# Attention layer 0: projection begun inside the last head, the next batch's transposes between its tiles; feed-forward stage written without a loop

## The chip, the cores and the metric

The kernel runs on one core of a Trainium2 chip. The metric is the device time in microseconds (us); the kernel before ran in 2813.58 us, the median of three runs (2812.09 to 2816.76). The core has a matrix engine (TensorE, PE in rows), three elementwise engines (VectorE or DVE, ScalarE or ACT, GpSimd or POOL) and a queue engine (SP) that issues most transfers. PE reads from SBUF and writes only into PSUM, here 8 banks of 128 x 512 fp32. DVE and ACT read and write both memories; GpSimd works in SBUF alone here.

## The reference, cut to what matters

Input x is 4 sequences (B) of 1024 tokens (T) of 512 features (D). Layer 0 is attention between two conditioned LayerNorms; layer 1 is attention and a feed-forward block whose weights are ternary and whose activations are rounded to 8 bits.

```python
# layer 0, for each of 4 sequences; 16 heads of 32
h   = gamma * layernorm(x) + beta                   # "front": gamma, beta from the condition
q, k, v = split(h @ Wqkv.T + bqkv)
out = (softmax(q @ k.T) / D ** 0.5) @ v
h1  = out @ Wp.T + bp + x                           # projection and residual
x   = gamma * layernorm(h1) + beta + h1             # "tail"
# layer 1
x = x + bitlinear(attention(bitlinear(adaln(x))), w_proj, b_proj)
x = x + bitlinear(gelu(bitlinear(adaln(x), w_fc1, b_fc1)), w_fc2, b_fc2)
```

## The kernel before

Three functions run one after the other: `layer0`, `layer1a` (attention of layer 1) and `layer1b` (feed-forward). Each engine has its own instruction stream, written out in Python; an engine works its stream strictly in order, and a `wait_ge` on a semaphore holds everything behind it.

`layer0` goes over the 4 batches b. In each: 16 units of q and k and 8 of v (L995, 12 matmuls each, made of high and low fp32r parts `h_hi`, `h_lo` of the front's output); then 16 heads (`Attention.run_pe`, `run_act`, `run_dve`, `run_pool`: `loop` calls `head` for k = 0 to 16, each with steps s = 0 to 7). In step s of head k PE computes two 128 x 512 score tiles (L428, PSUM banks 0 to 2 in a ring), ACT takes their exponentials (L508), and PE computes chunks of the row maxima for a head ahead (L414, banks 3 to 5, reduced by DVE at L547). There are none of these chunks left after step 1 of head 14, so banks 3 to 5 are free from there. Behind step 2 and inside step 6 come the products with the values (L448, banks 6 and 7), a copy by ACT (L517), 16 tiny matmuls that fold and transpose (L455) and the division by DVE (L564, L566), which puts a head's output into `tok`. POOL sums exponentials (L368, L374); four of the sums of a last pair are DVE's (L385, L390).

After the heads comes what this document calls the boundary. PE transposes `tok` (eight units of 4 transposes of 128 x 128, L1030), ACT and DVE copy half of them each into `oT` (L1144, L1440), and PE projects: 8 token tiles t, each of 4 matmuls k over 128 features, that is four heads each (L1037), into PSUM bank t. For each tile DVE adds the residual (L1451), computes the LayerNorm statistics (L1468, L1472) and their inverse root (L1454, L1456), ACT normalises (L1150), DVE multiplies by gamma (L1465), POOL adds beta to h1 (L908) and DVE adds both (L1475) into `xs`, which SP stores. POOL adds the bias `bp` to the residual ahead of it (L902). The semaphore `s_x1` counts the finished tiles. Then the front of the next batch: its input `xn` (normalised by DVE, L1202) is transposed by PE into eight PSUM banks (L936, units n = 4c + k for token half c and feature quarter k), each as soon as the tail has left that bank; ACT and DVE turn each into `h_hi` (L1061 and L1058), a full-precision copy in place (L1063 on ACT for c = 0, `exact`, L1209, on DVE for c = 1) and `h_lo` (L1216, function `rest`). ACT also takes squares of `xs` (L1083) and absolute sums of weight pieces (L1078) in this time. In the last batch there is no next front; instead the tail goes on with layer 1's first RMSNorm and its quantisation (L1459, L1478, L911, L1296).

`layer1b` goes over 32 tiles of 128 tokens as a software pipeline: `steps` calls a list of stages (offset, function) for each step n, in the order of the list. Steps n = -6 to 1 and 26 to 33 are written out; steps 2 to 25 are a loop of 6 rounds of 4 steps, in which n is a register and every slice that depends on n has an address computed at run time. In a step DVE finds the largest |h| (L2157, 2048 wide), makes six 128 x 1 values (L2164, L2176, L2170), turns matmul results into h (L2191, twice), rounds (L2181, L2198) and adds the residual (L2204); ACT scales and rounds (L2112, L2126), takes Gelu (L2122, twice), makes 8-bit values (L2131), scales a later tile (L2106) and copies (L2116); POOL modulates that later tile (L2047, L2051) and adds a bias (L2054).

## Time and profile before

| | |
|---|---|
| median of three runs | 2813.58 us |
| the profiled execution's own time | 2812.82 us |
| its span, first to last instruction | 2811.0 us |
| PE busy | 2632.5 us, 94% |
| DVE busy | 2185.9 us, 78% |
| ACT busy | 1826.0 us, 65% |
| POOL busy | 1922.1 us, 68% |
| mean granted TensorE clock | 0.981 of full speed |

A row of the timeline gives the start, the time taken, the engine, the source line and operation, what is written and read, and how many instructions are merged; in square brackets stands the idle time of the engine before it and what ended that. PE's matmuls are pipelined, so their durations overlap and the pace is read from the starts. In the rows fp32 data of 512 columns appears as two instructions per matmul, so the 32 matmuls of the projection are 64.

### The profile page before, as it was taken

Reading aid. Unit: us, or ns where it says so; the run is one execution under the profiler, and the core shown is the slowest. Engines: PE = TensorE matmul, PEld = TensorE weight load, DVE = VectorE, ACT = ScalarE, POOL = GpSimd, SP = SyncE. Lnnn points to the kernel's source line nnn. Section 1 sums busy time; section 2 is a strip of 40 time slices with the busy share of each in tenths; the row PEclk is TensorE's granted clock in tenths of the full one; section 3 lists DMA queues with packets and bytes.
Section 4 is the critical chain, followed back from the end, with each engine's and each line's share of the span. In section 5 each row is a group of like instructions: output and inputs, shape, how many; then the busy total and the mean of one; then the engine's idle time right before and its main releaser. Section 6 shows DMA issues by size and latency. Waiting matters only on the chain. (4 is left out here: it accounts for less than half of the span.)

```text
span 2811.0 us, 60795 instructions
## 1 busy us (share of the span) xinstructions
PE 2632.5 (94%) x21761; PEld 1461.6 (52%) x21761; DVE 2185.9 (78%) x4491; ACT 1826.0 (65%) x3298; POOL 1922.1 (68%) x1547
## 2 busy tenths in 40 slices
PE   7899999999999999999859998999899999987998
PEld 5655466554665547555325554555455445533443
DVE  5777678777887778877567778777877787758997
ACT  4366654665556655666556677667766776667886
POOL 0289724897259962699548986987789788965442
PEclk9999999999999999999979999999999999999999
DMA  6122443224432335223232313321432232245444
GB/s 233 39 58 58 143 127 114 58 58 147 129 97 62 85 116 164 74 58 103 75 80 53 85 34 106 81 59 31 117 81 58 50 99 58 59 181 162 100 101 108
DMA packets 168754, 260.29 MB, mean 93 GB/s; under 512 B 85388, under 2 KB 91668, under 8 KB 167576
## 3 DMA queue, kind: packets, MB, share of 16 engines
q1 hardware_dynamic: 166680, 250.27, 32.6%
q0 software_dynamic: 1792, 6.33, 0.6%
q8 instruction: 169, 2.77, 0.4%
q14 instruction: 113, 0.93, 0.1%
HBM read 99.15 MB, written 38.88 MB: 49 GB/s over the span
## 5 line engine op out<-in xcount | busy, mean ns | idle before, releaser
L547 DVE TENSOR_REDUCE a_mxs<-ps 128x1 f32<-128x512 f32 x2048 | 1268.8, 682 | 258.1 <-PE ps L414 255.7
L508 ACT ACTIVATE a_p<-ps 128x512 f32<-128x512 f32 x2048 | 1043.1, 605 | 204.3 <-PE ps L428 194.3
L368 POOL TENSOR_TENSOR a_sum<-a_p 128x512 f32<-128x512 f32 x736 | 939.9, 1287 | 204.0 <-PE ps L448 123.4
L414 PE MATMUL ps<-a_k,a_q 96*128 96x512 f32 x2048 | 856.3, 425 | 24.5 <-DVE a_mxs L547 20.9
L428 PE MATMUL ps<-a_q,a_k 98*128 98x512 f32 x2048 | 810.0, 418 | 18.5 <-ACT a_p L508 11.5
L448 PE MATMUL ps<-a_sum,a_unit 128*32 128x512 f32 x1536 | 654.0, 598 | 3.0 <-POOL a_sum L368 3.0
L374 POOL TENSOR_TENSOR a_sum<-a_sum,a_p 128x512 f32<-128x512 f32 x480 | 618.8, 1289 | 37.6
L448 PE MATMUL ps<-a_p,xv 128*32 128x512 f32 x3968 | 642.5, 598 | 0.0
L414 PEld LDWEIGHTS ps<-a_k,a_q 96*128 96x128 f32 x2048 | 389.8, 190 | 258.6 <-DVE a_mxs L547 105.5
L428 PEld LDWEIGHTS ps<-a_q,a_k 98*128 98x128 f32 x2048 | 384.1, 189 | 258.1 <-ACT a_p L508 162.0
L517 ACT ACTIVATE a_ots<-ps 128x512 f32<-128x512 f32 x256 | 152.8, 598 | 397.5 <-PE ps L448 396.4
L448 PEld LDWEIGHTS ps<-a_sum,a_unit 128*32 128x32 f32 x1536 | 135.6, 110 | 164.8 <-issue 129.1
L448 PEld LDWEIGHTS ps<-a_p,xv 128*32 128x32 f32 x3968 | 165.3, 110 | 101.3 <-issue 69.8
L564 DVE RECIPROCAL a_rec<-ps 128x4 f32<-128x4 f32 x256 | 45.2, 176 | 138.3 <-PE ps L455 138.3
L455 PEld LDWEIGHTS ps<-a_fold,a_ots 128*32 128x32 f32 x8192 | 98.4, 111 | 88.9 <-issue 85.0
L2074 PE MATMUL ps<-b_next_w,c_xqT 128*128 128x512 bf16 x512 | 118.7, 386 | 22.1 <-DVE c_h L2191 20.1
L2085 PE MATMUL ps<-b_next_w,c_hT 128*128 128x512 bf16 x512 | 117.2, 383 | 7.8 <-DVE b_next_x L2204 6.4
L455 PE MATMUL ps<-a_fold,a_ots 128*32 128x33 f32 x8192 | 118.9, 198 | 2.1 <-ACT a_ots L517 2.1
L2047 POOL TENSOR_TENSOR c_tk<-c_tk,b_next_mod 128x512 f32<-128x512 f32 x32 | 40.5, 1266 | 115.5 <-ACT c_tk L2106 115.5
L1037 PE MATMUL ps<-qh,ql 128*128 128x512 f32 x256 | 110.8, 593 | 3.3 <-ACT ql L1144 3.3
L908 POOL TENSOR_TENSOR kh<-kh,qh 128x512 f32<-128x512 f32 x32 | 40.6, 1270 | 83.4 <-ACT ps L1150 72.7
L2074 PEld LDWEIGHTS ps<-b_next_w,c_xqT 128*128 128x128 bf16 x512 | 48.2, 99 | 91.0 <-DVE c_h L2191 26.5
(251 smaller groups left out, 3049.1 us busy)
## 6 DMA issues: line engine op xcount, KB each, us to landing
a_q<-qh SPq DMA_DIRECT2D x256, 128.0 KB, 2.3
a_k<-kh SPq DMA_DIRECT2D x256, 128.0 KB, 2.4
a_q<-ql SPq DMA_DIRECT2D x128, 128.0 KB, 2.3
a_k<-kl SPq DMA_DIRECT2D x128, 128.0 KB, 2.4
x<-a_p SPq DMA_DIRECT2D x64, 256.0 KB, 2.1
a_p<-in_w_fc SPq DMA_DIRECT2D x12, 1024.0 KB, 8.0
kh<-in_x SPq DMA_DIRECT2D x4, 2048.0 KB, 14.4
a_p<-x SPq DMA_DIRECT2D x16, 512.0 KB, 5.8
```

The source lines that it names most:

```text
L368: pair = pool.tensor_tensor(tile, keys[0], keys[1], ALU.add)
L374: pool.tensor_tensor(tile, tile, keys[2], ALU.add).then_inc(self.s_sum, 1)
L414: pe.matmul(self.mx[self.mx_ring[at]], self.q[j][0:96, t * P:(t + 1) * P], self.k[j][0:96, half * HALF:(half + 1) * HALF], start=True, sto ...
L428: pe.matmul(self.st[self.st_ring[at]], self.k[j][0:98, kt * P:(kt + 1) * P], self.q[j][0:98, u * HALF:(u + 1) * HALF], start=True, stop=Tr ...
L448: mm = pe.matmul(self.ot[half % 2][HD * c:HD * (c + 1), :], weights, tile, start=r == rounds[0], stop=r == rounds[-1])
L455: mm = pe.matmul(self.ot[u][HD * c:HD * (c + 1), t * (HD + 1):(t + 1) * (HD + 1)], self.ots[:, u, t * P + HD * c:t * P + HD * (c + 1)], se ...
L508: act.activation(self.key_tile(u, kt), self.st[self.st_ring[CHUNKS * k + n]], ACT.Exp, scale=self.scale).then_inc(self.s_exp, 1)
L517: act.activation(self.ots[:, u, :], self.ot[u], ACT.Copy).then_inc(self.s_ots, 1)
L547: dve.reduce_max(self.mxs[:, k % 2, c:c + 1], self.mx[self.mx_ring[CHUNKS * k + c]], axis=AX.X).then_inc(self.s_mxr, 1)
L1037: mm = pe.matmul(ps[:, t, :], oT[:, k, t * P:(t + 1) * P], wp[:, k, :], start=k == 0, stop=k == KC - 1)
L2074: mm = pe.matmul(f1[:, j, :], xqT[:, r % 2, k, :], w1[:, k, j * HALF:(j + 1) * HALF], start=k == 0, stop=k == KC - 1)
L2085: mm = pe.matmul(f2, hT[:, r % 2, k, :], w2[:, k, :], start=k == 0, stop=k == FC - 1)
```

## The change

1. In heads 14 and 15 PE transposes six of the eight units of `tok` (`tokens`, those of heads 0 to 11) into banks 3 to 5, between score tiles, and DVE copies them to `oT` (`extra` in DVE's stream). From step 4 of head 15 to the end of the loop PE does seven matmuls of the projection (`projected`). The last two units of `tok` follow behind the loop, with two more matmuls between them; ACT copies these two, and its `roots` now comes before them.
2. The projection's tiles go to other banks (`Y_BANK`), and so do the next q, k and v units. From tile 3 on, PE puts one transpose unit of the next batch's front behind each tile; the front uses banks 3, 4, 5, 0, 3, 4, 5, 1, and its units wait for the multiplication by gamma (`s_gm`) or for `rest` of the unit before in that bank. ACT now makes the full-precision copy for all eight units, DVE's `exact` is only for batch 0. ACT and DVE begin on the front at t = 4 and t = 6 of the tail's loop.
3. The multiplication by gamma now writes `xs` out of PSUM, and the last addition of the tail is POOL's.
4. `layer1b` writes all steps out; the order of the stages in a step stays.

```diff
+        s_gm = sem("gamma")
         s_rr, s_xr, s_vl = sem("root_inv"), sem("x_rooted"), sem("v_last")
-        tail_home = lambda b, t: ps[:, t, :] if t < 6 or b == B - 1 else xs[:, t, :]
         UN = 2 * KC
+        Y_BANK = (3, 4, 5, 0, 1, 2, 6, 7)
+        tail_home = lambda b, t: ps[:, Y_BANK[t], :] if t < 6 or b == B - 1 else xs[:, t, :]
+        FRONT_BANK = lambda b: (3, 4, 5, 0, 3, 4, 5, 1) if b else tuple(range(UN))
+        TOKENS = [(k, c) for c in range(2) for k in range(KC - 1)] + [(KC - 1, 0), (KC - 1, 1)]
+        T_BANK = (3, 4, 5, 3, 4, 5, 6, 7)
+        EARLY = len(TOKENS) - 2
+        TOKENS_AT = {(14, 4): 0, (14, 5): 1, (14, 7): 2, (15, 0): 3, (15, 1): 4, (15, 3): 5}
+        COPIED_AT = {(14, 5): 0, (14, 6): 1, (15, 0): 2, (15, 1): 3, (15, 2): 4, (15, 4): 5}
+        PART_AT = {(15, 4): ((0, 0),), (15, 5): ((0, 1),), (15, 7): ((0, 2),), (16, 0): ((1, 0),), (16, 1): ((1, 1),),
+                   (16, 2): ((1, 2),), (16, 6): ((2, 0),)}
...
-                    for t in range(TT + 4 if last else TT):
+                    for t in range(TT + 4 if last else TT + 1):
                         if t < TT:
                             pool.wait_ge(s_zt, TT * b + t + 1)
+                            pool.wait_ge(s_xb, TT * b + t + 1)
                             pool.tensor_tensor(h1[:, t, :], h1[:, t, :], mod_r[:, 1, :], ALU.add).then_inc(s_hb, 1)
+                        if 1 <= t <= TT:
+                            pool.wait_ge(s_gm, TT * b + t)
+                            pool.wait_ge(s_hb, TT * b + t)
+                            pool.tensor_tensor(xs[:, t - 1, :], xs[:, t - 1, :], h1[:, t - 1, :], ALU.add).then_inc(s_x1, 1)
...
-                        if prior is not None:
-                            if n < 6:
-                                pe.wait_ge(s_x1, TT * prior + n + 1 + 1)
-                            else:
-                                pe.wait_ge(s_h1, TT * prior + n + 1)
+                        if b and n < 4:
+                            pe.wait_ge(s_gm, TT * (b - 1) + n + 1)
+                        elif b and n < 7:
+                            pe.wait_ge(s_trD, UN * b + n - 4 + 1)
+                        elif b:
+                            pe.wait_ge(s_gm, TT * (b - 1) + Y_BANK.index(FRONT_BANK(b)[n]) + 1)
                         for i in range(4):
-                            mm = pe.transpose(ps[:, n, i * P:(i + 1) * P], xn[:, 4 * c + i, k * P:(k + 1) * P], ident)
+                            mm = pe.transpose(ps[:, FRONT_BANK(b)[n], i * P:(i + 1) * P], xn[:, 4 * c + i, k * P:(k + 1) * P], ident)
                         mm.then_inc(s_tr, 1)
+
+                def tokens(b, i):
+                    k, c = TOKENS[i]
+                    if i == 0:
+                        pe.wait_ge(att.s_mxr, CHUNKS * H * (b + 1) + att.MX_CREDIT)
+                    if i < EARLY:
+                        pe.wait_ge(att.s_o, 2 * H * b + 2 * NJ * (KC - 1) + 2)
+                    else:
+                        pe.wait_ge(att.s_o, 2 * H * (b + 1) + c + 1)
+                    if 3 <= i < EARLY:
+                        pe.wait_ge(s_opD, EARLY * b + i - 3 + 1)
+                    for n in range(4):
+                        mm = pe.transpose(ps[:, T_BANK[i], n * P:(n + 1) * P], tok[:, 4 * c + n, k * P:(k + 1) * P], ident)
+                    mm.then_inc(s_op, 1)
+
+                def projected(b, t, k):
+                    if (t, k) == (0, 0):
+                        pe.wait_ge(s_late, 48 * (b + 1))
+                    if t < 3 and k == 0:
+                        pe.wait_ge(s_opD, EARLY * b + 3 + t + 1)
+                    if (t, k) == (3, 0):
+                        pe.wait_ge(att.s_exp, CHUNKS * H * (b + 1) + att.EXP_CREDIT)
+                    if (t, k) == (4, 0):
+                        pe.wait_ge(s_opD, EARLY * (b + 1))
+                    if t >= 6 and k == 0:
+                        pe.wait_ge(s_opA, 2 * b + t - 6 + 1)
+                    if t in (0, 4) and k == KC - 1:
+                        pe.wait_ge(s_opA, 2 * b + t // 4 + 1)
+                    mm = pe.matmul(ps[:, Y_BANK[t], :], oT[:, k, t * P:(t + 1) * P], wp[:, k, :], start=k == 0, stop=k == KC - 1)
+                    if k == KC - 1:
+                        mm.then_inc(s_y, 1)
...
-                    att.run_pe(pe, b)
-                    pe.wait_ge(att.s_o, 2 * H * (b + 1) + 2)
-                    for n, (c, k) in enumerate(HALVES):
-                        for i in range(4):
-                            mm = pe.transpose(ps[:, n, i * P:(i + 1) * P], tok[:, 4 * c + i, k * P:(k + 1) * P], ident)
-                        mm.then_inc(s_op, 1)
-                    pe.wait_ge(s_opA, KC * (b + 1))
-                    pe.wait_ge(s_opD, KC * (b + 1))
-                    pe.wait_ge(s_late, 48 * (b + 1))
+                    def extra(k, s):
+                        if (k, s) in TOKENS_AT:
+                            tokens(b, TOKENS_AT[k, s])
+                        for t, c in PART_AT.get((k, s), ()):
+                            projected(b, t, c)
+                    att.run_pe(pe, b, extra)
+                    tokens(b, EARLY)
+                    projected(b, 2, 1)
+                    tokens(b, EARLY + 1)
+                    projected(b, 2, 2)
                     for t in range(TT):
-                        for k in range(KC):
-                            mm = pe.matmul(ps[:, t, :], oT[:, k, t * P:(t + 1) * P], wp[:, k, :],
-                                           start=k == 0, stop=k == KC - 1)
-                        mm.then_inc(s_y, 1)
+                        for c in range(KC - 1 if t < 3 else 0, KC):
+                            projected(b, t, c)
+                        if not last and t >= 3:
+                            front(b + 1, (t - 3,))
                     if not last:
-                        front(b + 1, b)
+                        front(b + 1, range(5, UN))
...
+                        to, at = h_hi[:, k, c * HALF:(c + 1) * HALF], ps[:, FRONT_BANK(b)[n], :]
+                        if c and b == 0:
+                            act.wait_ge(s_trG, k + 1)
+                            act.activation(to, at, ACT.Copy).then_inc(s_trA, 1)
                             continue
                         act.wait_ge(s_tr, UN * b + n + 1)
-                        act.activation(to, ps[:, n, :], ACT.Identity,
+                        act.activation(to, at, ACT.Identity,
                                        bias=mod_col(b, 1, k), scale=mod_col(b, 0, k)).then_inc(s_trA, 1)
-                        act.activation(ps[:, n, :], ps[:, n, :], ACT.Identity,
+                        act.activation(at, at, ACT.Identity,
...
-                    for n, (c, k) in enumerate(HALVES):
-                        if k % 2 == 0:
-                            act.wait_ge(s_op, UN * b + n + 1)
-                            act.activation(oT[:, k, c * HALF:(c + 1) * HALF], ps[:, n, :], ACT.Copy).then_inc(s_opA, 1)
                     if not last:
                         roots(b + 1)
+                    for i in range(EARLY, len(TOKENS)):
+                        k, c = TOKENS[i]
+                        act.wait_ge(s_op, len(TOKENS) * b + i + 1)
+                        act.activation(oT[:, k, c * HALF:(c + 1) * HALF], ps[:, T_BANK[i], :], ACT.Copy).then_inc(s_opA, 1)
...
-                        if not last and t == 6:
-                            modulate(b + 1, range(2))
+                        if not last and 4 <= t:
+                            modulate(b + 1, (t - 4,))
                     if not last:
-                        modulate(b + 1, range(2, UN))
+                        modulate(b + 1, range(5, UN))
                         act.wait_ge(s_wsum, done(b + 1) + 2)
...
+                    def extra(k, s):
+                        if (k, s) in COPIED_AT:
+                            i = COPIED_AT[k, s]
+                            n, c = TOKENS[i]
+                            dve.wait_ge(s_op, len(TOKENS) * b + i + 1)
+                            dve.tensor_copy(oT[:, n, c * HALF:(c + 1) * HALF], ps[:, T_BANK[i], :]).then_inc(s_opD, 1)
+                    att.run_dve(dve, b, spare, extra)
...
-                        if t >= TT and not last:
-                            modulate(b + 1, t - TT)
                         if 2 <= t < TT + 2:
-                            home = tail_home(b, t - 2)
                             dve.wait_ge(s_zt, TT * b + t - 1)
-                            cht.mark(dve.tensor_tensor(home, home, mod_r[:, 0, :], ALU.mult))
+                            dve.tensor_tensor(xs[:, t - 2, :], tail_home(b, t - 2), mod_r[:, 0, :], ALU.mult).then_inc(s_gm, 1)
+                        if t >= 6 and not last:
+                            rest(b + 1, t - 6)
                         if t < TT:
                             dve.wait_ge(s_h1, TT * b + t + 1)
                             cht.mark(dve.bn_stats(st1[:, t, :], h1[:, t, :]))
-                        if t < TT + 2:
+                        if t < TT:
                             cht.wait_alone()
-                        if t < TT:
                             dve.bn_aggr(mv[1][:, t, :], st1[:, t, :]).then_inc(s_var1, 1)
-                        if 2 <= t < TT + 2:
-                            dve.wait_ge(s_hb, TT * b + t - 1)
-                            dve.tensor_tensor(xs[:, t - 2, :], home, h1[:, t - 2, :], ALU.add).then_inc(s_x1, 1)
                         if last and 5 <= t < TT + 5:
                             dve.wait_ge(s_xr, t - 5 + 1)
-                            dve.tensor_tensor(xv[:, t - 5, :], ps[:, t - 5, :], g1[:, 0, :], ALU.mult).then_inc(s_n1, 1)
...
+                    if not last:
+                        for n in range(4, UN):
+                            rest(b + 1, n)
...
-        def steps(eng, stages, before_loop=lambda: None):
-
-            def step(n, r, every):
+        def steps(stages, before_third=lambda: None):
+
+            for n in range(FIRST, N + 2):
+                if n == 2:
+                    before_third()
                 for o, f in stages:
-                    if every or 0 <= n + o < N:
-                        f(n + o, (r + o) % UNROLL)
-            for n in range(FIRST, 2):
-                step(n, n % UNROLL, False)
-            before_loop()
-            with eng.Fori(0, LOOPS) as i:
-                for r in range(UNROLL):
-                    step(UNROLL * i + 2 + r, (2 + r) % UNROLL, True)
-            for n in range(2 + UNROLL * LOOPS, N + 2):
-                step(n, n % UNROLL, False)
+                    if 0 <= n + o < N:
+                        f(n + o, (n + o) % UNROLL)
```

PE at the end of batch 0, from the last step of head 15 to the first q unit. `a_q`, `a_k` rows are scores, `a_p`, `a_sum` rows products with values, `ps<-ident,tok` transposes of `tok`, `ps<-qh,ql` the projection (the two names are the memory of Wp and `oT`), `ps<-ident,kl` the next front. Before:

```order
L455 MATMUL ps<-a_fold,a_ots 32x33 x32
L1030 MATMUL ps<-ident,tok 128x128 x32
L1037 MATMUL ps<-qh,ql 128x512 x32
L936 MATMUL ps<-ident,kl 128x128 x32
L995 MATMUL ps<-a_h_hi,a_q 128x512 x4
```

and in the changed kernel, in two pieces, the steps of head 15 from step 3 and then what follows the last products with values:

```order
L428 MATMUL ps<-a_q3,a_k3 128x512 x2
L967 MATMUL ps<-ident,tok 128x128 x4
L428 MATMUL ps<-a_q3,a_k3 128x512 x2
L983 MATMUL ps<-qh,ql 128x512
L428 MATMUL ps<-a_q3,a_k3 128x512 x2
L983 MATMUL ps<-qh,ql 128x512
L428 MATMUL ps<-a_q3,a_k3 128x512 x2
```

```order
L455 MATMUL ps<-a_fold,a_ots 32x33 x16
L983 MATMUL ps<-qh,ql 128x512
L967 MATMUL ps<-ident,tok 128x128 x4
L983 MATMUL ps<-qh,ql 128x512
L967 MATMUL ps<-ident,tok 128x128 x4
L983 MATMUL ps<-qh,ql 128x512 x8
L953 MATMUL ps<-ident,kl 128x128 x4
L983 MATMUL ps<-qh,ql 128x512 x4
L953 MATMUL ps<-ident,kl 128x128 x4
```

Seven projection matmuls and six transpose units stand between the last heads' matmuls, and only the last four front units (16 transposes) are behind the projection. On DVE, tile 7 of the tail in batch 0 read before (the row of L1451 is the residual, the last one the addition that goes to POOL):

```order
L1451 TENSOR_TENSOR kh<-ps,kh 128x512
L1454 RECIPROCAL a_rs1<-a_sd1 128x1
L1456 TENSOR_SCALAR a_nm<-a_mv1,a_rs1 128x1
L1465 TENSOR_TENSOR ps<-ps,qh 128x512
L1468 BN_STATS a_st1<-kh 128x6
L1472 BN_AGGR a_mv1<-a_st1 128x2
L1475 TENSOR_TENSOR a_p<-ps,kh 128x512
```

and reads now, with what each waits for:

```order
L1507 TENSOR_TENSOR kh<-ps,kh 128x512 [waits a_xb,a_y]
L1510 RECIPROCAL a_rs1<-a_sd1 128x1 [waits a_sd1_ok]
L1512 TENSOR_SCALAR a_nm<-a_mv1,a_rs1 128x1 [waits a_v_tail]
L1518 TENSOR_TENSOR a_p<-ps,qh 128x512 [waits a_zt]
L1270 TENSOR_TENSOR a_h_lo_75<-ps,a_h_hi_76 128x4x128 [waits a_trF,a_trA]
L1523 BN_STATS a_st1<-kh 128x6 [waits a_h1]
```

The last addition is gone from DVE's tile, and one `rest` of the next front stands in its place.

## Rows read from the trace of the kernel before

**Rows 1.** Timeline of PE, batch 0, from the last products to the next q unit

```profile
340.66 0.59 PE L448 MATMUL ps<-a_sum,a_unit 128*32 128x512 f32 x1 [0.59 <-POOL a_sum L368]
...
343.53 3.71 PE L1030 MATMUL ps<-ident,tok 128*128 128x128 f32 x32 [0.64 <-DVE tok L566]
348.07 27.70 PE L1037 MATMUL ps<-qh,ql 128*128 128x512 f32 x64 [0.83 <-ACT ql L1144]
...
383.20 1.19 PE L995 MATMUL ps<-a_h_hi,a_q 128*128 128x512 f32 x4 [2.67 <-ACT a_h_hi L1061]
```

**Rows 2.** Timelines of PE and ACT in head 15, eight score tiles

```profile
323.41 0.96 PE L428 MATMUL ps<-a_q,a_k 98*128 98x512 f32 x3
324.66 2.46 PE L428 MATMUL ps<-a_q,a_k 98*128 98x512 f32 x5 [0.28 <-ACT a_p L508]
...
324.02 4.02 ACT L508 ACTIVATE a_p<-ps 128x512 f32<-128x512 f32 x8
```

**Rows 3.** Timeline of DVE, heads 14 and 15 and boundary of batch 0

```profile
321.97 1.70 DVE L385 TENSOR_TENSOR a_sum<-a_p 128x512 f32<-128x512 f32 x1
...
327.80 0.29 DVE L566 SCALAR_TENSOR_TENSOR tok<-ps,a_rec 128x128 f32<-128x128 f32 x1
...
349.23 4.60 DVE L1202 TENSOR_SCALAR kl<-kl,a_mv,a_rs 128x512 f32<-128x512 f32 x8
...
364.54 0.66 DVE L1475 TENSOR_TENSOR a_p<-ps,kh 128x512 f32<-128x512 f32 x1
```

**Rows 4.** Timeline of ACT, boundary of batch 0

```profile
365.51 1.91 ACT L1078 ACTIVATE a_ots<-a_p 128x2048 bf16<-128x2048 f32 x1
...
376.25 0.78 ACT L1061 ACTIVATE a_h_hi<-ps,a_mod_p 128x512 fp32r<-128x512 f32 x1 [0.46 <-PE ps L936]
376.93 0.74 ACT L1063 ACTIVATE ps<-ps,a_mod_p 128x512 f32<-128x512 f32 x1
```

**Rows 5.** Timeline of DVE, tail of the last batch, its first and last instruction

```profile
1375.91 0.69 DVE L1451 TENSOR_TENSOR kh<-ps,kh 128x512 f32<-128x512 f32 x1 [3.87 <-PE ps L1037]
...
1415.82 0.69 DVE L1296 TENSOR_REDUCE a_am<-xv 128x1 f32<-128x512 f32 x1 [0.54 <-POOL xv L911]
```

**Rows 6.** Windows: length, PE, PEld, DVE, ACT, POOL busy, granted clock, DMA

```profile
333.00:338.00 5.00, 5.00 (x52) 1.47 (x51) 1.86 (x4) 1.68 (x4) 2.66 (x3) 0.66 0.01 3
```

**Rows 7.** Timeline of DVE, feed-forward: the loop's first step and the first step behind it

```profile
2567.25 2.29 DVE L2157 TENSOR_REDUCE c_am<-c_h 128x2048 f32 x1 [0.39 <-ACT c_h L2122]
...
2756.94 2.27 DVE L2157 TENSOR_REDUCE c_am<-c_h 128x1 f32<-128x2048 f32 x1
...
2762.07 1.27 DVE L2181 TENSOR_SCALAR c_xq<-c_tk 128x512 bf16<-128x512 f32 x1
...
2763.85 0.90 DVE L2198 TENSOR_SCALAR c_hq<-c_h 128x512 bf16<-128x512 f32 x1
...
2765.33 2.27 DVE L2157 TENSOR_REDUCE c_am<-c_h 128x1 f32<-128x2048 f32 x1
```

**Rows 8.** Timeline of ACT, feed-forward, from the loop into the written-out steps

```profile
2752.38 0.72 ACT L2112 ACTIVATE c_tk<-c_tk,c_am 128x512 f32<-128x512 f32 x1 [0.93 <-DVE c_am L2170]
...
2759.75 0.72 ACT L2112 ACTIVATE c_tk<-c_tk,c_am 128x512 f32<-128x512 f32 x1 [0.40 <-DVE c_am L2170]
...
2762.27 1.99 ACT L2122 ACTIVATE c_h<-c_h 128x1024 f32<-128x1024 f32 x2
```

**Rows 9.** Timelines of DVE, ACT and POOL in written-out steps ahead of the loop

```profile
2557.55 0.42 DVE L2181 TENSOR_SCALAR c_xq<-c_tk 128x512 bf16<-128x512 f32 x1
...
2564.91 1.02 DVE L2181 TENSOR_SCALAR c_xq<-c_tk 128x512 bf16<-128x512 f32 x1
...
2557.75 1.99 ACT L2122 ACTIVATE c_h<-c_h 128x1024 f32<-128x1024 f32 x2
...
2564.37 1.28 POOL L2054 TENSOR_TENSOR b_next_x<-b_next_x,b_next_b 128x512 f32<-128x512 f32 x1
```

**Rows 10.** Timeline of DVE at the end of the kernel

```profile
2802.18 0.75 DVE L2204 SCALAR_TENSOR_TENSOR b_next_x<-ps,c_am,b_next_x 128x512 f32<-128x512 f32 x1 [3.78 <-issue]
```

69 lines of the change are left out of this document (33 added, 36 removed).

## The prediction

> **What bounds the kernel now.** The page comes first: PE is busy for 94% of the span, so what frees PE counts and what adds to it costs, except where PE only seems busy. The timeline of PE at the end of a batch shows the first such place. In batch 0 the last product waits 0.59 us for POOL's sum, the transposes 0.64 us for DVE, the projection 0.83 us for ACT, and the first q unit 2.67 us for ACT's `h_hi` [rows 1]. From that last product's wait to the q unit at 383.20 are 42.5 us, of which the projection is 27.5 (64 instructions, 0.43 us apart, so 0.86 us a matmul and 3.44 a tile) and the eight units of `tok` 3.7 (0.46 us each) [rows 1]. The other boundaries repeat these figures.
>
> The second place is inside head 15. PE's rows for eight score tiles start at 323.41 and end at about 327.05: 3.64 us. The first three are issued some 0.24 us apart, so eight need 1.9 us; the other five come at ACT's pace, whose eight exponentials take 4.02 us [rows 2]. PE shows as busy and has 1.7 us to spare in such a group. There are three of them from head 14, step 3 on, where no maxima are left to compute: 5.2 us a batch.
>
> The third is the feed-forward stage. Its 24 looped steps run from 2567.25 to 2756.94, 7.90 us each [rows 7]. What limits them is a ring, not one engine: ACT rounds h and does Gelu, DVE takes the maximum and the small factors, ACT goes on. In the loop ACT's L2112, which heads the ring, starts after 0.93 us of waiting for DVE's L2170 [rows 8].
>
> **Part 1: work moved into the heads.** Six transposed units (6 x 0.46 = 2.8 us) and seven matmuls (7 x 0.86 = 6.0 us) leave the boundary. Two units fall into the first group and three into the second: 0.9 and 1.4 us, under the 1.7 to spare, and free, since PE may be three tiles ahead of ACT. The third group gets one unit and two matmuls, 2.2 us, 0.5 too much. Three more matmuls (2.6 us) stand ahead of the last products, where PE waited 0.59 us before: net 2.0. So the folds, which began at 341.5, begin at 344.0. From there PE does two folds (0.3 us each), two units (0.9), seven matmuls to the end of tile 2 (6.0), and five tiles of 3.44 with a front unit of 0.46 behind each (19.5): 371. The last three front units end at 372.5. That is PE's own floor, 10.7 us under 383.20.
>
> DVE must keep up in head 15. The division there ended at 328.1 [rows 3]. Four copies of 0.6 us now stand ahead of it. Idle stretches of 0.4 to 0.5 us absorb some; the sum L385, which took 1.70 us because POOL was in a sum of its own [rows 3], ends at the same moment when it starts later; 0.7 us is left. The division ends at 328.8, and the product that needs it starts at 329.05, two rounds of 0.86 us behind the fold: nothing is added, by 0.2 us.
>
> **Part 2: the front's chain.** DVE goes through a tile in 3.44 us at PE's pace; without L1475 (0.6) and a wait of 0.3 it is 2.5 us. It begins behind the normalisation, 4.60 us [rows 3], at about 351, with three tiles waiting, and has caught up at tile 5. PE's first front unit waits 1 us for gamma; tile 7 ends at 371.5. ACT is what is late next: each of the eight units now takes L1061 and L1063, 1.33 us [rows 4], where four took 0.5 us for a copy. With normalisation, root and square it has 2.9 us of work a tile, and in two tiles 2.1 us more for L1078 [rows 4]. Taken tile by tile: DVE has the statistics of tile 7 at 374.6; ACT squares and modulates unit 3 until 376.9 and normalises tile 7 until 377.6; PE's front units 6 and 7 wait for `rest` of unit 2 (377.1) and end at 378.1, where the q unit starts. The last `rest` (383.6) is needed by the third q unit at 385.4: hidden, by 1.8 us. POOL has two operations of 1.27 us in 3.9 us; its lateness moves stores and squares only. So 383.20 becomes 378.1, and 0.2 us of waiting inside the first q unit goes: **5.3 us at each of three boundaries, 16 us**. The bounds are PE's floor, 10.7 us each, and nothing, if ACT and DVE hold PE until the old time.
>
> DVE's multiplication by gamma for tiles 6 and 7 reads two SBUF operands while POOL runs. The nearest row is L385, 1.70 us against 0.66 for L1475 with POOL idle [rows 3]; the schedule has 0.6 us for each. The Trainium skill (SBUF — State Buffer, section "SBUF: two separate sides") says that such a DVE operation and a GpSimd one take a shared port pair exclusively, so that one waits out the other; the row agrees. By that rule alone each could wait out a whole POOL operation, and the sum would be some 4 us smaller over three boundaries.
>
> **Part 3: the last batch.** DVE bounds its tail: 40.6 us from the first residual to the last maximum [rows 5]. Tiles 0 to 2 now come some 6 us earlier. A full tile takes DVE 3.7 us without the addition of 0.6, and POOL, with three operations, 3.8: POOL becomes the pace. Gone through in the same way, the last maximum comes 6.8 us earlier: **7 us**. Bounds: 4, if POOL is held up at each tile, to 10.
>
> **Part 4: the feed-forward stage.** L2164, L2176 and L2170 write through computed addresses in the loop. From the loop into the written-out steps ACT's L2112 follows after 7.37 us, not 7.90, and its wait falls from 0.93 to 0.40 [rows 8]. So a ring of 7.4 us is shown. DVE alone needs 7.06: the step from 2756.94 to 2765.33 without the 0.85 and 0.48 us that L2181 and L2198 took too long [rows 7, 9]. L2181 also meets POOL's third operation: POOL's ended at 2565.65, L2181, begun at 2564.91, at 2565.93, and took 1.02 us instead of 0.42 [rows 9]. POOL's third ends 5.9 us behind the Gelu [rows 9], and the Gelu ends 7.3 us after the maximum's start [rows 7, 8]; so in steps of S it ends at 13.2 - S into the next, L2181 0.3 us behind it, and DVE has 1.6 more: S = 15.1 - S, or 7.55. That saves 24 x 0.35 = 8.5 us, and the first step behind them 0.4: **9 us**. Bounds: 12 (the ring alone) and nothing.
>
> The Trainium skill (Advanced Engine Details and Errata, "Control Flow Timing") gives a compare and branch 108 ns. By that the loop's six rounds cost under 1 us, and the sum would be 8 us smaller. The rows speak for more: the interval shortens within a step.
>
> **Part 5: the clock.** In head 15 of batch 0 the granted clock was 0.66 on average over 5 us, that is partly at the lower level, 1.2 GHz [rows 6], in products that follow tiles at ACT's pace; batch 3 has the same. Each cost some 1.6 us. PE now has work in those gaps. I count half: **1.6 us**.
>
> **Sum.** 16 + 7 + 9 + 1.6 = 33.5 us. The profiled execution took 2812.8, so 2779.3; the median of the runs is 0.8 higher: 2780.
>
> **Rivals.** (a) Without the loop only its branches are saved: 24.6 + 1 us, 2788. For it: the ring could be paced by more than the small operations. Against: rows 8. Chance 0.12. (b) The front's chain on ACT, or POOL in DVE's way, holds PE, and layer 0 gives half: 12 + 9, 2792. For it: only 1.8 us between the last `rest` and its need, 0.2 for the division. 0.13. (c) Layer 0 gives more: 10 us a boundary, near PE's floor, and both clock falls gone, 2764. 0.10. (d) Each feed-forward step meets POOL twice, as that of 8.39 us did [rows 7]: 24 x 0.49 = 12 us more than before in place of 9 less, 2801. Against: POOL had four additions in a row there, which only the steps behind the loop have. 0.04. (e) Slower: straight-line code arrives late. DVE stood 3.78 us near the end with no engine named [rows 10]. One such gap in each of 24 steps decides from 33.5 / 24 = 1.4 us; at 2 us the time is 2828. Against: layer 0 is straight-line already, and its q unit's 4 matmuls follow one another in 1.19 us [rows 1]. 0.03. The rest, 0.58, is the forecast, in 2774 to 2786.
>
> **Numbers.** A measurement of this kernel can tell about 0.2%, 5.6 us, from no change. The range leaves out (d), (e) and most of (c): 2769 to 2793. Faster 0.96, within 0.2% 0.01, slower 0.03.
>
> **What would show it.** The q unit 5 us nearer to the last heads, its wait for ACT gone; L2157's starts 7.5 to 7.6 us apart with L2181 at 0.7 to 1.0 us; the third score group of head 15 longer by 0.5 us, the others as before; the last maximum 7 us earlier. The prediction is wrong if PE waits for L566 in head 15, if front units wait for `rest` by more than 1 us each, or if steps stay at 7.9 us.

## The result, and the profile after

The changed kernel ran in 2795.3 us, the median of four runs (2792.4 to 2797.7), against 2814.4 for the kernel before on the same chip: a ratio of 0.9932, with a 95% interval of 0.9914 to 0.9949. It is faster, by 19 us. The prediction was 2780, in 2769 to 2793: the direction was right, and the gain nearly 60% of the 33.5 us forecast. The profiled execution took 2797.68 us, with a span of 2795.9: 15.1 us under the span before. It is the longest of the changed kernel's four runs (two are near 2797 us, two near 2793), so this pair of traces shows 4 us less than the medians; the working below goes by the pair. The page begins:

```profile
span 2795.9 us, 59973 instructions
PE 2621.9 (94%) x21716; PEld 1469.8 (53%) x21761; DVE 2162.2 (77%) x4455; ACT 1830.6 (65%) x3302; POOL 1964.9 (70%) x1579
```

Lines have moved: L1037 is now L983, L936 L953, L995 L1048, L1202 L1256, L1216 L1270, L902 L912, L1465 L1518, L2157 L2204, L2181 L2228. PE in the third group of score tiles of head 15, in batch 0:

```profile
330.77 0.74 PE L428 MATMUL ps<-a_q,a_k 98*128 98x512 f32 x2
331.35 0.60 PE L967 MATMUL ps<-ident,tok 128*128 128x128 f32 x4
...
333.68 1.02 PE L983 MATMUL ps<-qh,ql 128*128 128x512 f32 x2
334.14 1.04 PE L428 MATMUL ps<-a_q,a_k 98*128 98x512 f32 x2
335.11 0.46 PE L455 MATMUL ps<-a_fold,a_ots 128*32 128x33 f32 x32
```

From 330.77 to the folds (L455) are 4.34 us, where the group in [rows 2] took 3.64; the extra 0.7 us buys a transposed unit and two matmuls. This part went as forecast. The timeline of PE at the boundary, which answers to [rows 1], did not:

```profile
343.10 0.48 PE L455 MATMUL ps<-a_fold,a_ots 128*32 128x33 f32 x32
...
347.65 7.03 PE L983 MATMUL ps<-qh,ql 128*128 128x512 f32 x16
357.97 0.82 PE L953 MATMUL ps<-ident,kl 128*128 128x128 f32 x4 [3.28 <-DVE a_p L1518]
358.58 5.14 PE L983 MATMUL ps<-qh,ql 128*128 128x512 f32 x8
...
364.00 3.60 PE L983 MATMUL ps<-qh,ql 128*128 128x512 f32 x8
...
375.18 0.60 PE L953 MATMUL ps<-ident,kl 128*128 128x128 f32 x4
377.64 0.66 PE L953 MATMUL ps<-ident,kl 128*128 128x128 f32 x4 [1.86 <-DVE a_h_lo L1270]
380.45 1.97 PE L953 MATMUL ps<-ident,kl 128*128 128x128 f32 x8 [2.15 <-DVE a_h_lo L1270]
382.06 2.06 PE L1048 MATMUL ps<-a_h_hi,a_q 128*128 128x512 f32 x4
383.92 1.85 PE L1048 MATMUL ps<-a_h_hi,a_w_lo 128*128 128x512 f32 x4
385.61 1.08 PE L1048 MATMUL ps<-a_h_lo,a_q 128*128 128x512 f32 x4
```

The folds begin at 343.10 (forecast 344.0) and tile 3 is done before 355. Then PE stands 3.28 us for the first multiplication by gamma, and tile 4, eight instructions, takes 5.14 us where the next takes 3.60. The last front units wait 1.86 and 2.15 us for `rest`, and the q unit starts at 382.06, only 1.1 us earlier than before, with its first four matmuls in 2.06 us where they took 1.19. Its third group of matmuls starts at 385.61; before, it started at 385.59, so by then nothing is left of the gain. Windows of the same stretch (length, then PE, PEld, DVE, ACT and POOL busy, granted clock, DMA share and GB/s) show what the long rows are:

```profile
354.00:358.00 4.00, 0.72 (x3) 0.06 (x2) 3.64 (x12) 1.93 (x4) 1.26 (x1) 1.00 0.43 166
358.00:363.00 5.00, 5.00 (x11) 2.50 (x12) 2.88 (x8) 2.76 (x7) 4.88 (x4) 0.66 0.00 0
363.00:375.00 12.00, 12.00 (x38) 5.87 (x37) 7.66 (x19) 9.54 (x18) 5.07 (x5) 1.00 0.07 7
382.00:386.00 4.00, 4.00 (x12) 3.21 (x12) 2.63 (x5) 4.00 (x8) 3.72 (x3) 0.55 0.99 376
```

Behind the idle 354 to 358 the granted clock averages 0.66 over 5 us, and in the q unit 0.55 over 4, so it is partly at the lower level, 1.2 GHz. The trace of the kernel before has no such stretch at a boundary, though PE waits 1.03 and 2.67 us there: an idle gap is not enough by itself, as e11 and e12 show again below. DVE's timeline tells why gamma was late, with one row of POOL's beside it:

```profile
345.76 7.03 DVE L1256 TENSOR_SCALAR kl<-kl,a_mv,a_rs 128x512 f32<-128x512 f32 x8
352.70 0.68 DVE L1507 TENSOR_TENSOR kh<-ps,kh 128x512 f32<-128x512 f32 x1
...
357.14 0.68 DVE L1518 TENSOR_TENSOR a_p<-ps,qh 128x512 f32<-128x512 f32 x1
...
379.71 0.68 DVE L1270 TENSOR_TENSOR a_h_lo<-ps,a_h_hi 128x512 fp32r<-128x512 f32 x1
```

```profile
340.24 10.43 POOL L912 TENSOR_TENSOR kh<-kh,qh 128x512 f32<-128x512 f32 x8
```

The eight normalisations of the next input took 7.03 us, not 4.60 [rows 3], beside POOL's additions of `bp`. Tile 0's residual waited for them. The later boundaries repeat it: the q units start at 723.75 (before 724.45) and 1065.08 (before 1065.00). Over three boundaries and the batches between them nothing was gained. Taken apart: from the folds behind head 15 to the q unit are 38.9 us at each boundary, 2.8 less than before (41.69); the q unit's first two groups take 1.0 to 1.2 us more; and from the third group to the next batch's folds are 2.1 and 2.6 us more, the price of the matmuls that now stand in the heads (forecast 2.5).

The other two parts went as forecast. The last maximum of the last batch and the feed-forward maxima, both on DVE:

```profile
1409.13 0.69 DVE L1350 TENSOR_REDUCE a_am<-xv 128x1 f32<-128x512 f32 x1 [0.53 <-POOL xv L926]
...
2560.85 2.29 DVE L2204 TENSOR_REDUCE c_am<-c_h 128x1 f32<-128x2048 f32 x1 [0.26 <-ACT c_h L2169]
...
2606.04 2.27 DVE L2204 TENSOR_REDUCE c_am<-c_h 128x1 f32<-128x2048 f32 x1
...
2611.16 0.95 DVE L2228 TENSOR_SCALAR c_xq<-c_tk 128x512 bf16<-128x512 f32 x1
...
2741.27 2.27 DVE L2204 TENSOR_REDUCE c_am<-c_h 128x1 f32<-128x2048 f32 x1
2749.34 2.27 DVE L2204 TENSOR_REDUCE c_am<-c_h 128x1 f32<-128x2048 f32 x1
```

The last maximum comes 6.7 us earlier than in [rows 5]; as the q unit of this batch started no earlier, all of it was gained in the last batch. The 24 steps that were a loop take 180.42 us, 7.52 each (before 189.69, 7.90), and the step behind them 8.07, not 8.39 [rows 7].

The spans differ by 15.1 us: layer 0 (to its last maximum) 6.7 shorter, layer 1's attention 0.4 longer, from the first to the last 2048-wide maximum 9.7 shorter, and 0.9 longer behind it.

### The profile page after: what moved, and what is told of

The parts are those of the page before. It is cut to its first block and busy times, and to the rows that moved or that the text cites. A ratio compares the mean times of both kernels' runs of the same rounds, so it can differ in the third digit from the quotient of the medians.

```text
span 2795.9 us, 59973 instructions
## 1 busy us (share of the span) xinstructions
PE 2621.9 (94%) x21716; PEld 1469.8 (53%) x21761; DVE 2162.2 (77%) x4455; ACT 1830.6 (65%) x3302; POOL 1964.9 (70%) x1579
## 5 line engine op out<-in xcount | busy, mean ns | idle before, releaser
L455 PEld LDWEIGHTS ps<-a_fold,a_ots 128*32 128x32 f32 x8192 | 98.0, 110 | 90.2 <-issue 85.4
L983 PE MATMUL ps<-qh,ql 128*128 128x512 f32 x256 | 121.2, 612 | 0.0
L455 PE MATMUL ps<-a_fold,a_ots 128*32 128x33 f32 x8192 | 118.5, 198 | 0.4 <-ACT a_ots L517 0.4
L1731 POOL TENSOR_TENSOR xv<-xv,kh 128x512 f32<-128x512 f32 x32 | 40.4, 1277 | 71.3 <-ACT xv L1847 42.3
```

What stands on the lines that cost most here:

```text
L455: mm = pe.matmul(self.ot[u][HD * c:HD * (c + 1), t * (HD + 1):(t + 1) * (HD + 1)], self.ots[:, u, t * P + HD * c:t * P + HD * (c + 1)], se ...
L983: mm = pe.matmul(ps[:, Y_BANK[t], :], oT[:, k, t * P:(t + 1) * P], wp[:, k, :], start=k == 0, stop=k == KC - 1)
```

## Experiments

Two theories were tried against each other. A: the boundary is DVE's. The normalisation meets POOL, the tail starts late, PE's idle time is followed by a half clock, and the order of `rest` behind tile 7 sets the q unit. B: something else holds PE (the chain through ACT, the load of the chip), and DVE's start matters little. Each kernel is the changed one with the edit named (e12 is the kernel before with one); all but the changed one were timed beside the kernel before in one of three groups (2813.2, 2812.9 and 2812.8 us). The starts are from one trace of each.

| run | median us | ratio to before, 95% | folds to q unit, us (batches 0, 1, 2) | q unit of batch 1 | of batch 3 | last maximum of layer 0 |
|---|---|---|---|---|---|---|
| before | 2812.8 to 2813.2 | 1 | 41.7, 41.7, 41.7 | 383.20 | 1065.00 | 1415.82 |
| changed | 2795.3 | 0.9932 (0.9914 to 0.9949) | 39.0, 38.9, 38.9 | 382.06 | 1065.08 | 1409.13 |
| e1_bp_split | 2783.6 | 0.9895 (0.988 to 0.991) | 34.2, 34.2, 34.2 | 377.98 | 1050.64 | 1395.11 |
| e2_filler | 2786.1 | 0.9897 (0.9881 to 0.9912) | 36.5, 36.5, 36.5 | 379.55 | 1054.41 | 1397.97 |
| e3_ff_loop | 2809.3 | 0.9985 (0.9976 to 0.9994) | 39.0, 38.9, 38.0 | 384.68 | 1067.57 | 1413.12 |
| e4_norm_split | 2789.4 | 0.9913 (0.99 to 0.9927) | 36.4, 36.1, 35.8 | 380.93 | 1058.22 | 1401.72 |
| e5_shift | 2797.5 | 0.995 (0.9936 to 0.9963) | 38.5, 38.4, 38.4 | 382.27 | 1065.99 | 1410.84 |
| e6_no_part | 2788.3 | 0.9914 (0.9901 to 0.9928) | 38.0, 38.3, 38.6 | 378.44 | 1055.63 | 1401.41 |
| e7_split_filler | 2775.4 | 0.9868 (0.9853 to 0.9883) | 33.4, 33.4, 33.4 | 375.08 | 1044.13 | 1387.53 |
| e8_dve_add | 2802.2 | 0.9964 (0.995 to 0.9977) | 39.9, 41.0, 39.9 | 383.43 | 1069.10 | 1416.34 |
| e9_late_part | 2774.3 | 0.9869 (0.9852 to 0.9886) | 35.0, 35.0, 35.0 | 375.62 | 1044.38 | 1388.06 |
| e10_split_shift | 2769.8 | 0.9853 (0.984 to 0.9867) | 30.6, 30.6, 30.6 | 372.56 | 1037.80 | 1381.39 |
| e11_shift_only | 2783.5 | 0.9903 (0.9888 to 0.9918) | 33.7, 35.4, 35.4 | 378.15 | 1052.58 | 1395.72 |
| e12_ff_only | 2800.7 | 0.9968 (0.9955 to 0.9981) | 41.7, 41.7, 41.7 | 381.20 | 1065.57 | 1415.56 |

Ten of these kernels (all but before, e6, e9 and e12) have the same code up to the folds behind head 15 of batch 0, and yet these folds start anywhere from 341.70 (e7) to 345.66 us (e3). The start of a q unit carries this difference, the time from the folds to it does not.

### e1: POOL's additions out of the normalisation's way

```diff
                     for t in range(TT):
+                        if t == 4 and not last:
+                            pool.wait_ge(s_z, TT * (b + 2))
                         pool.tensor_tensor(h1[:, t, :], h1[:, t, :], bp, ALU.add).then_inc(s_xb, 1)
```

> POOL adds bp to four tiles, waits for DVE's eight normalisations, and adds it to the other four. Theory A (POOL's additions beside DVE's normalisation are what made it 7.03 us in place of 4.60; the first front unit's wait of 3.28 us and the half clock behind it follow from that): the normalisation takes 4.6 us again, the wait of the first front unit falls by 2.4 us to about 0.9, tile 4 takes 3.44 us and not 5.14, and the q units start 2.4 to 4.1 us earlier at each of three boundaries: 7 to 12 us off 2795. Theory B (the chain through DVE and ACT behind tile 7 sets the q unit, whatever the start of the tail): the wait of the first front unit falls too, but the last front units' waits of 1.86 and 2.15 us grow by as much; under 2 us in all.

Measured: 11.7 us faster than the changed kernel. DVE's row, then PE's two:

```profile
346.47 3.74 DVE L1258 TENSOR_SCALAR kl<-kl,a_mv,a_rs 128x512 f32<-128x512 f32 x8
```

```profile
355.57 0.63 PE L955 MATMUL ps<-ident,kl 128*128 128x128 f32 x4 [0.17 <-DVE a_p L1520]
...
373.55 0.66 PE L955 MATMUL ps<-ident,kl 128*128 128x128 f32 x4 [1.86 <-DVE a_h_lo L1272]
376.36 1.97 PE L955 MATMUL ps<-ident,kl 128*128 128x128 f32 x8 [2.15 <-DVE a_h_lo L1272]
```

The normalisation takes 3.74 us, 0.47 each, which is less than in the kernel before: there it met POOL's last additions too. The wait of 3.28 falls to 0.17 and the half clock behind it is gone: tile 4 takes 3.60 us. From the folds to the q unit are 34.2 us at all three boundaries, in place of 38.9. The waits of 1.86 and 2.15 us are unchanged to the hundredth, so they don't depend on when the tail starts. Theory B fell, for it wanted them longer. The low clock in the q unit stays too: its third group starts 2.53, 3.40 and 3.56 us behind its first in the three batches.

### e2 and e7: work in PE's idle time

Matmuls into banks that are overwritten later, `filler(bank, 3)` ahead of front unit 0 (e2 only) and `filler(bank, 2)` ahead of units 5 and 6, behind a wait (`s_h1`) until DVE has read the bank:

```diff
+                def filler(to, count):
+                    for i in range(count):
+                        pe.matmul(ps[:, to, :], oT[:, 0, 0:P], wp[:, 0, :], start=True, stop=True)
```

> The changed kernel with three idle-time matmuls on PE ahead of the first front unit and two each ahead of front units 5 and 6, into banks that are overwritten later; nothing else moves. Theory A (the two half-clock stretches at a boundary come from PE's idle time just before them): granted clock 1.00 in both stretches, tile 4 in 3.44 us (1.7 less), first q unit's twelve matmuls 2 us faster: 2 to 3.7 us at each boundary, 6 to 11 us in all. Theory B (the low clock has another cause, such as the load of the whole chip): the stretches stay, no gain, or up to 2 us loss from the seven matmuls where they outlast the waits.

> POOL's additions divided as in e1_bp_split, and two idle-time matmuls on PE ahead of front units 5 and 6, none ahead of unit 0. Theory A (the remaining half-clock stretch comes from the waits of 1.86 and 2.15 us): the stretch is gone at all three boundaries, last eight transposes in 1.1 and not 1.97 us, the first q unit's twelve matmuls 2 us faster: 2 to 3 us a boundary, 2774 to 2778. Theory B (the low clock follows from the load, not from the waits): 2783, as without.

The first q unit of batch 1 in e7:

```profile
375.08 1.18 PE L1054 MATMUL ps<-a_h_hi,a_q 128*128 128x512 f32 x4
...
377.03 1.09 PE L1054 MATMUL ps<-a_h_lo,a_q 128*128 128x512 f32 x4
```

The unit's third group starts 1.95 us behind its first; in the changed kernel 3.55 (382.06 to 385.61). Windows of e2 over the two places of low clock:

```profile
358.00:363.00 5.00, 5.00 (x18) 2.67 (x19) 3.77 (x12) 2.77 (x6) 4.94 (x4) 1.00 0.00 0
379.00:383.00 4.00, 4.00 (x23) 3.42 (x22) 2.58 (x4) 4.00 (x7) 3.45 (x4) 1.00 1.05 404
```

The clock stays at the upper level in both, with the other engines doing what they did. The useless matmuls make the kernel 9.2 us faster (e2), and 8.2 us faster on top of e1 (e7, forecast 2774 to 2778). Not all of the 8.2 is theirs: e7's first folds already start 2.1 us before e1's, in the same code, and the three boundaries with their q units give 6.0. So the low clock came with PE's idle time, and the load around it was not enough to bring it about.

### e4: half of the normalisation behind the tail's start

```diff
-                        normalize(ch, b + 1)
+                        normalize(ch, b + 1, range(4))
...
+                        if 3 <= t < TT - 1 and not last:
+                            normalize(ch, b + 1, (t + 1,))
```

> DVE normalises four tiles of the next input ahead of the tail and one each behind tiles 3 to 6, POOL's additions as in the changed kernel. The tail begins 3.5 us earlier (half of 7.03). Theory A: the first front unit's wait of 3.28 us is gone, tile 4 at full clock: 3 to 5 us at each boundary, 9 to 14 us in all, a little less where the late normalisations (0.6 us each) stand in DVE's chain. Theory B (the chain behind tile 7 sets the q unit): 0 to 2 us, or slower by the 0.6 us that stand between the statistics and the next residual.

Only 5.9 us were gained, where theory A wanted 9 to 14 and B at most 2. The first half did not take 3.5 us:

```profile
347.16 5.20 DVE L1257 TENSOR_SCALAR kl<-kl,a_mv,a_rs 128x512 f32<-128x512 f32 x4
```

Four normalisations beside POOL take 1.30 us each, and alone the same instruction takes 0.47 (e1). POOL's additions take 1.30 each here (10.43 for 8) and 1.24 where no normalisation runs beside them (4.97 for 4 in e1). DVE goes at POOL's pace, one instruction to an addition, as if each waited one out, and POOL loses little. This is the row that sizes the meeting.

### e5 and e11: the order of the front's work on ACT and DVE

e11 changes only the order, as below. e5 has e4's and e1's division too (POOL waits for four normalisations), and calls `rest` one step earlier still, for unit t - 4 from t = 4 on:

```diff
-                        if not last and 4 <= t:
-                            modulate(b + 1, (t - 4,))
+                        if not last and 3 <= t:
+                            modulate(b + 1, (t - 3,))
...
-                        if t >= 6 and not last:
-                            rest(b + 1, t - 6)
+                        if t >= 5 and not last:
+                            rest(b + 1, t - 5)
```

> DVE normalises four tiles ahead of the tail and one behind each of tiles 3 to 6; POOL adds bp to four tiles, waits for those four normalisations, then to the rest; ACT turns front unit t - 3 in its step t (before: t - 4), DVE's rest of unit t - 4 in its step t (before: t - 6). Theory A (what holds the q unit, once the tail starts in time, is that rest of units 1 and 2 stands behind tile 7's statistics in DVE's order): no front unit waits over 0.5 us, the last ends some 2 us behind tile 7, so the q unit starts near 372 to 374 in batch 1, 8 to 10 us earlier than in the changed kernel and 4 to 6 us earlier than with POOL's additions divided alone; no half clock at the boundary; the third q unit may wait 1 us for ACT. 2766 to 2772 us. Theory B (ACT has no room for a unit at each tile: 2.9 us of 3.9, and 1.9 more at two tiles): ACT's normalisation of the tail comes late, gamma and then PE's front units wait, and the result is within 3 us of POOL's additions divided alone, 2781 to 2787.

> The changed kernel with only the order of the front's work changed (ACT unit t - 3 in step t, DVE rest of unit t - 5 in step t). Theory A: the wait of 3.28 us at the first front unit and the half clock behind it stay; the waits of 1.86 and 2.15 us fall to 0 and under 1.5, so the q unit starts 3 to 4 us earlier than 382.06, and without the half clock in it another 2 us are gained: 12 to 17 us off 2795, 2778 to 2783. Theory B (ring through ACT): no gain or slower, 2795 to 2800.

e5 was no faster than the changed kernel: the forecast of 2766 to 2772 was wrong by 25 us, and theory B's 2781 to 2787 by 10. DVE, ACT and then PE in it:

```profile
364.04 0.69 DVE L1273 TENSOR_TENSOR a_h_lo<-ps,a_h_hi 128x512 fp32r<-128x512 f32 x1 [2.44 <-ACT ps L1119]
364.65 1.61 DVE L1259 TENSOR_SCALAR kl<-kl,a_mv,a_rs 128x512 f32<-128x512 f32 x1
```

```profile
367.22 0.20 ACT L1209 ACTIVATE a_sd<-a_mv 128x1 f32<-128x1 f32 x1 [2.59 <-DVE a_mv L1531]
```

```profile
379.16 3.36 PE L955 MATMUL ps<-ident,kl 128*128 128x128 f32 x16 [6.30 <-DVE kl L1259]
```

Unit t - 4 is made by ACT in its step t - 1, behind the root for tile t - 1; with `rest` of that unit ahead of tile t's statistics, DVE waits 2.44 us for ACT, and ACT then waits 2.59 us for DVE's statistics: a ring through both engines. And three of the four late normalisations of this batch take 1.61 us beside POOL (in the same batch of e4 they took 0.54 to 0.77). PE waits 6.30 us for the last of them. e11 leaves one step between ACT and DVE and has no ring: 11.9 us faster than the changed kernel, though its first front unit waits as long as before:

```profile
359.32 0.63 PE L953 MATMUL ps<-ident,kl 128*128 128x128 f32 x4 [3.28 <-DVE a_p L1518]
359.79 3.60 PE L983 MATMUL ps<-qh,ql 128*128 128x512 f32 x8
...
374.84 1.04 PE L953 MATMUL ps<-ident,kl 128*128 128x128 f32 x8
377.30 1.09 PE L953 MATMUL ps<-ident,kl 128*128 128x128 f32 x8 [1.43 <-DVE a_h_lo L1270]
378.15 1.17 PE L1048 MATMUL ps<-a_h_hi,a_q 128*128 128x512 f32 x4
```

One wait of 1.43 is left of 1.86 and 2.15; from front unit 4 to the q unit are 3.3 us where the changed kernel has 6.9 (375.18 to 382.06), and the q unit's first four matmuls take 1.17 us again. The forecast that the half clock at tile 4 stays was wrong for this boundary only: with the same wait of 3.28 us, tile 4 took 3.60. At the other two the granted clock behind the wait was 0.66 over 5 us again, and from the folds to the q unit were 35.4 us, not 33.7. So the same wait is followed by the lower level at one boundary and not at another; what decides was not found. The kernel landed at 2783.5, just above the 2778 to 2783 forecast.

### e6 and e9: is the projection worth starting in the heads?

```diff
-        PART_AT = {(15, 4): ((0, 0),), (15, 5): ((0, 1),), (15, 7): ((0, 2),), (16, 0): ((1, 0),), (16, 1): ((1, 1),),
-                   (16, 2): ((1, 2),), (16, 6): ((2, 0),)}
+        PART_AT = {}
...
-                        for c in range(KC - 1 if t < 3 else 0, KC):
+                        for c in range(KC):
```

> The changed kernel without the nine projection matmuls that stand ahead of, between and just behind the last heads' work: the whole projection is done after the last transposes of the tokens. Six transposed units stay in the heads. Theory A (PE's time saved by them was given back as waiting for DVE at the first front unit): the six or so us of matmuls come back in front of tile 3, the wait of 3.28 us there is gone, PE's clock does not fall there, and the kernel is only 0 to 4 us slower per three boundaries plus up to 4 in the last batch: 2795 to 2803. Theory B (each matmul moved is worth its 0.86 us): 7 x 0.86 = 6 us at each of four batches less 0.5 and 2.0 that they cost in the heads, some 14 us slower: 2809.

> In batches 0 to 2 the whole projection stands behind the heads (as in e6_no_part), in the last batch its first nine matmuls stay where the change put them; POOL adds bp to three tiles, waits for the normalisation, then to five; ACT turns front unit t - 3 in its step t, DVE's rest of unit t - 5 in its step t. Theory A (the matmuls inside the last heads put the division and the normalisation 2.65 us later on DVE, and the front units' last waits come from the order of rest): the folds near 340.4, the normalisation 3.8 us from 343, tile 7 at 372.5, the q unit near 375, no half clock: 2766 to 2771. Theory B (starting the projection early is worth its 1.2 us of PE once DVE is in time): this is 3 to 5 us slower than e10_split_shift.

e9 is more than this edit: it has e11's order and POOL's additions divided (three, wait, five) too, and takes the matmuls out in batches 0 to 2 only.

e6 was 7 us faster than the changed kernel: outside what either theory gave. DVE and PE in it:

```profile
343.11 8.53 DVE L1253 TENSOR_SCALAR kl<-kl,a_mv,a_rs 128x512 f32<-128x512 f32 x8
351.55 0.68 DVE L1504 TENSOR_TENSOR kh<-ps,kh 128x512 f32<-128x512 f32 x1
```

```profile
356.81 0.63 PE L952 MATMUL ps<-ident,kl 128*128 128x128 f32 x4
```

Without those matmuls the folds come at 340.45, not 343.10, DVE's normalisation begins 2.65 us earlier and, though it meets more of POOL's additions (8.53 us), the tail starts 1.15 us earlier; PE arrives at the first front unit when gamma is done, so there is neither wait nor half clock at that place (1.00 from 356 to 372). The waits of 1.86 and 2.15 us and the low clock behind them stay (0.66 from 378 to 383). In the last batch, which has no front, the same matmuls are worth 1.7 us: from its q unit to PE's first matmul behind the tail it lasts 347.06 us in e6 and 345.33 with them. e9 and e10 ask the question again with DVE in time: e10, which keeps the matmuls in the heads, is 4.5 us faster than e9, which has them only in the last batch. That is theory B's 3 to 5 us; theory A's 2766 to 2771 missed, at 2774.3. Starting early is worth 1.5 us a boundary by these medians if DVE is ready to follow, and 2.2 by the traces (q unit of batch 3 at 1037.80 against 1044.38), with the difference in how POOL's additions are divided in it; it cost 3.6 in batch 1 (382.06 against 378.44) where DVE was not ready.

### e8: the last addition back on DVE

```diff
-                        if 1 <= t <= TT:
...
-                            pool.tensor_tensor(xs[:, t - 1, :], xs[:, t - 1, :], h1[:, t - 1, :], ALU.add).then_inc(s_x1, 1)
...
+                        if 2 <= t < TT + 2:
...
+                            dve.tensor_tensor(xs[:, t - 2, :], xs[:, t - 2, :], h1[:, t - 2, :], ALU.add).then_inc(s_x1, 1)
```

> The changed kernel with the tail's last addition (0.6 us a tile) back on DVE, everything else as changed. Theory A (DVE's chain sets when rest of units 1 and 2 is done): rest 2 is two additions later, 1.2 to 1.8 us, so each boundary 1.5 to 3 us longer, and the last batch, DVE's too, 0 to 4 us: 2800 to 2808. Theory B (with two operations a tile POOL is DVE's rival for the shared port, and the addition was no gain): 2792 to 2797.

6.8 us slower than the changed kernel, as A wanted: the wait for the second `rest` is 3.25 us, not 2.15, and the last batch, measured as in e6, lasts 348.5 us, not 345.3.

### e3 and e12: the feed-forward stage alone

e3 is the changed kernel with `layer1b` of before; e12 is the kernel before with `layer1b` of the change.

> Layer 0 as changed, the feed-forward stage with its loop as before. If the traces are read rightly (feed-forward 240.2 us from first to last maximum before, 230.5 us after, its end 0.9 us longer) this is 8 to 9.5 us slower than the changed kernel, about 2804; if only the branches were saved, 1 to 2 us slower; if layer 0's gain is what the medians show and feed-forward gives less, 3 to 6 us.

> Layer 0 as before, the feed-forward stage written without a loop as in the changed kernel. If the step period falls from 7.90 to 7.5 us as the trace of the changed kernel shows, 24 x 0.4 less 0.9 at the end: 8.5 to 10 us faster than before, about 2804. If the two parts of the change are worth what e3_ff_loop says (it was 14 slower than the changed kernel), 12 to 15 us faster. If only the branches, 1 to 2 us.

e12 is 12.1 us faster than before, e3 14.0 slower than the changed kernel, both more than the traces gave (8.5 to 10, and 8 to 9.5). In the traces the stage itself is what was forecast: from the first to the last maximum of h 230.45 us in e12 and 230.47 in the changed kernel, 240.16 before and 240.72 in e3. The rest stands ahead of the stage, in code that is the same: the first such maximum starts at 2547.61 in e12 and 2552.41 before. All but 0.3 us of that arises in layer 1a (the last maximum of layer 0 is at 1415.56 and 1415.82), and some of it is the clock. Before, then e12:

```profile
1440.00:1460.00 20.00, 17.21 (x62) 7.78 (x61) 16.48 (x28) 11.66 (x18) 9.36 (x8) 0.83 0.54 119
```

```profile
1440.00:1460.00 20.00, 17.00 (x65) 7.59 (x63) 17.53 (x33) 12.75 (x19) 11.98 (x10) 0.91 0.53 119
```

The same stretch of code, 0.3 us apart in the two, had 0.83 of the clock in one kernel and 0.91 in the other. Layer 0 shows it too: behind nearly the same waits (1.03 and 2.67, 1.02 and 2.68 us) the q unit of batch 3 had a granted clock of 1.00 before and 0.57 over 4 us in e12. Over all the kernels the time from layer 0's last maximum to the first 2048-wide one, in code that no edit but the loop's touches, is 1132.05 to 1137.84 us. So two kernels can differ by some 5 us for work that neither changed, and of the differences between the medians above, those under that size are no proof by themselves; the times from folds to q unit are. What decides which it is was not tried.

### e10: the best version

e1's edit and e11's together.

> The changed kernel with POOL's additions of bp divided (four, wait, four), ACT's front unit t - 3 in its step t and DVE's rest of unit t - 5 in its step t, so rest of units 1 and 2 is ready two operations behind tile 7. Theory A: tile 7 at 371.1 as with the additions divided alone, front unit 5 without a wait, unit 6 with under 1.5 us, q unit near 374.5 and not 378, no half clock at the boundary: 10 to 14 us off 2783.6, 2769 to 2774. Theory B (ACT cannot take a unit a tile so early; the ring between ACT's unit, DVE's rest and the statistics, which gave 2797 when rest came one step earlier still, closes here too): 2785 to 2795.

```profile
369.25 1.04 PE L955 MATMUL ps<-ident,kl 128*128 128x128 f32 x8
371.71 1.09 PE L955 MATMUL ps<-ident,kl 128*128 128x128 f32 x8 [1.42 <-DVE a_h_lo L1272]
372.56 1.18 PE L1050 MATMUL ps<-a_h_hi,a_q 128*128 128x512 f32 x4
```

2769.8 us, 25.5 under the changed kernel and 43 under the one before. That is at the fast end of theory A's 2769 to 2774; the q unit starts 30.6 us behind the folds at all three boundaries. The windows from 354 to 380 show a granted clock of 1.00 throughout.

## Why the prediction was wrong, step by step

**The step that failed** is the term "5.3 us at each of three boundaries, 16 us". In batch 0 it measured 1.1 us up to the q unit, and the q unit's first two groups then took 1.2 us longer than before (3.55 against 2.39): nothing in all. Inside it the cost that was wrong is the normalisation's, 4.60 us, which measured 7.03 beside POOL, and the clock behind PE's waits was put at nothing. From the folds to the q unit the forecast had 34.1 us (344.0 to 378.1) and 38.96 were measured. There were four errors, shown in batch 0:

1. "It begins behind the normalisation, 4.60 us, at about 351." The normalisation took 7.03 us and ended at 352.7, so the first front unit waited 3.28 us and not 1: 2.3 us. The step that moved the normalisation 3.5 us earlier, from 349.23 to 345.76, also moved it into POOL's additions, which start when the heads end, as before. I took its duration from a row that stood almost behind them. e1 and e4 show this: 0.47 each apart from POOL, 1.30 beside it. The rule of the Trainium skill that the prediction weighed for gamma (SBUF — State Buffer, "SBUF: two separate sides") speaks of DVE operations in a 2-port mode as well as of those with two operands in SBUF; the measured 1.30 agrees with a wait for a whole addition, though no run shows in which mode these normalisations ran. The other direction of the rule is not borne out: POOL's eight additions took 10.43 us where eight times 1.24 are 9.9, so POOL lost some 0.1 us, and not 0.47, to each of the four that it met. I had applied it to two multiplications, one of which took 1.23 to 1.25 us at each boundary of e10; both took 0.68 to 0.69 at every boundary of the changed kernel.
2. The clock behind that wait: tile 4 in 5.14 us, not 3.44: 1.7 us. The prediction counted only falls that would vanish. Those in head 15 are gone in this trace, and two came at each boundary.
3. The chain from tile 7 to the q unit was forecast 6.6 us long (371.5 to 378.1) and measured 6.9 (375.18 to 382.06): 0.3 us, so its length was right. Its cause was not: the prediction had units 6 and 7 wait for `rest` of unit 2 because ACT was late. In the trace ACT holds DVE up there for only 0.27 us; what set it is DVE's order, in which `rest` of unit 1 stands behind tile 7's residual and `rest` of unit 2 behind its statistics as well. e11 shortens the chain from 6.9 to 3.3 us by order alone, so the 6.6 us were not needed. The prediction's own sign of being wrong, waits for `rest` of more than 1 us each, was all but there in its own schedule: the last front units end at 378.1 and not at their floor of 372.5, so PE stands 5.6 us.
4. The q unit at the lower level behind those waits: 1.6 us (3.55 against 1.95 in e7). The forecast had the idle time in front of it and no price for it.

The first three make 4.3 of the 4.9 us from folds to q unit; the other 0.6 lie in the projection up to the end of tile 3, 11.6 us against 10.9. The folds themselves came 0.9 us earlier than forecast. So at the q unit's third group 5.6 us a boundary are missing, about the whole term.

Over the kernel the sum was 33.5 us (its terms add to 33.6) and the spans differ by 15.1. Layer 0 was to give 24.6 and gave 6.7, so 17.9 are missing there; the feed-forward stage gave 8.8 of 9; and layer 1a, which was not changed, took 0.4 more.

**Part 1** was right within 1 us in every size (folds 343.10 against 344.0, third group 0.7 longer against 0.5, no wait for L566) and wrong in worth: PE time freed ahead of a DVE chain was given back as waiting (e6). **Part 3**, 7 us: measured 6.7. **Part 4**, 9 us: 24 steps of 7.52 against a forecast of 7.55, 9.3 us, the step behind them 0.3, and 0.9 lost behind the last maximum: 8.7 (8.8 from the first maximum on). The 0.9 need not belong to the change: that end took 19.3 us here, and 18.5 to 21.0 in other kernels with the same code for it (18.43 before). L2228 beside POOL took 0.83 us in the median, in 0.7 to 1.0 as said. The rivals of the loop (only branches, POOL met twice, late code) are out. That POOL's third operation sets 7.5 us and not 7.4 is argued from the rows; no run took it away. **Part 5**, 1.6 us: the two falls in head 15 are gone (1.00 from 332 to 340 and from 1340 to 1360), but e12, which has the layer 0 of before, lacks them there too and has one in batch 1 instead, so the change is not shown to have removed them. Rival (b), layer 0 gives half, had the right engines, "POOL in DVE's way", and its time, 2792, is nearest to the result; that is partly luck, for layer 0 gave 6.7 us and not 12, and the margins it named (1.8 us for the last `rest`, 0.2 for the division) are not the ones that broke.

## What to carry to other kernels

When an edit moves an instruction earlier, read what the other engines do at its new place before taking its old duration: here a 4.6 us block became 7.0 because it arrived while POOL was still adding. Freeing the busiest engine pays only as far as the chain that must follow it is ready, and an idle gap of some 2 to 3 us on PE can, though not each time, cost half its length again in the clock behind it. In a tail shared by several engines, put what another engine waits for ahead of bookkeeping, and leave a full step between two engines that feed each other. And when kernels differ by a few us, compare one stretch from the same event to the same event before comparing medians.

## What the runs showed of the hardware

- A DVE tensor_scalar of 128x512 fp32 in SBUF took 0.47 us alone and 1.30 us in a row beside GpSimd additions of 1.30 us (1.24 without it). Single ones between POOL's operations, in batch 0, took 0.54 to 0.77 us in e4 and 0.70 to 1.61 in e5.
- Idle stretches of PE of 3.28, or of 1.86 and 2.15 us close together, were followed by stretches with a mean granted clock of 0.66 and 0.55; with matmuls that do nothing useful in them it was 1.00, and the kernel 6 to 9 us faster. The 3.28 us were not always followed by it (e11: one boundary of three), and waits of 1.03 and 2.67 us were followed by 1.00 in the kernel before and by 0.57 in batch 3 of e12, in the same code.
- Unchanged code of layer 0 and 1a took 4.8 us more in one kernel than in another, with granted clocks of 0.83 and 0.91 in the same stretch.
